# A transformer layer with experts on one core: when the second phase's first weights are sent for, and where ScalarE sends for second weights

## The reference

```
h   = gelu(x @ w1[e] + b1[e])        # 256 -> 1024, for every expert e
eo  = h @ w2[e] + b2[e]              # 1024 -> 256
out = sum over the 2 experts chosen for each token, weighted
```

## Time and profile before

| what | value |
|---|---|
| median of 3 runs | 795.15 us (794.45 to 796.68) |
| profiled execution, whole time | 792.84 us |
| its span, first to last instruction | 791.1 us |
| mean granted TensorE clock in it | 0.974 |
| TensorE busy | 740.1 us, 94% of the span |
| VectorE, ScalarE, GpSimd busy | 51%, 48%, 30% |

### The profile page before, as it was taken

The page is one execution under the profiler, slowest core; times in us unless marked ns, Lnnn a source line. Parts: engine busy times, 40 slices in busy tenths (PEclk is TensorE's granted clock), DMA queues, the critical chain, the costliest instruction groups (busy, mean ns, idle before and its releaser), DMA issues. The chain is left out here.

```text
span 791.1 us, 14690 instructions
## 1 busy us (share of the span) xinstructions
PE 740.1 (94%) x5275; PEld 504.9 (64%) x5275; DVE 402.5 (51%) x974; ACT 380.0 (48%) x776; POOL 238.3 (30%) x432
## 2 busy tenths in 40 slices
PE   6889999999999999999997799996999999999983
PEld 4444544555455545545663677895899999999931
DVE  4577777767666777565677453664111011011125
ACT  3325456655656657587753456332433333433303
POOL 8313400112353322424643153202222222222115
PEclk9999999999999999999997899998999999999998
DMA  8968200702046112323227826568699999999663
GB/s 273 289 163 233 83 1 4 201 3 83 1 121 203 49 19 59 106 74 109 56 109 243 263 89 237 179 215 299 187 322 336 331 318 321 344 323 316 200 209 124
DMA packets 95152, 140.29 MB, mean 177 GB/s; under 512 B 11855, under 2 KB 81077, under 8 KB 92597
## 3 DMA queue, kind: packets, MB, share of 16 engines
q1 hardware_dynamic: 78533, 109.95, 44.1%
q10 hardware_dynamic: 12896, 19.92, 7.4%
q0 software_dynamic: 3648, 9.45, 3.3%
HBM read 110.65 MB, written 28.65 MB: 176 GB/s over the span
## 5 line engine op out<-in xcount | busy, mean ns | idle before, releaser
L1450 DVE TENSOR_REDUCE neg_part_max<-work 128x1 f32<-128x512 f32 (+4 forms) x368 | 212.8, 625 | 79.1 <-PE work L906 40.0
L1220 ACT ACTIVATE arena<-score_pair 128x1024 f32<-128x1024 f32 (+2 forms) x224 | 179.8, 839 | 86.6 <-PE score_pair L939 51.0
L906 PE MATMUL work<-arena 96*128 96x77 bf16 (+4 forms) x640 | 119.2, 280 | 9.1 <-DVE neg_part_max L1450 3.0
L936 PE MATMUL score_pair<-arena 99*128 99x512 bf16 (+2 forms) x448 | 113.4, 336 | 0.0
L959 PE MATMUL out_acc<-arena 128*32 128x512 f32 (+4 forms) x896 | 107.3, 517 | 0.6 <-ACT arena L1232 0.5
L829 PE MATMUL score_pair<-arena 128*128 128x256 f32 x432 | 97.6, 379 | 0.0
L1380 DVE TENSOR_TENSOR arena<-score_pair,arena 128x256 f32<-128x256 f32 x27 | 11.5, 425 | 166.8 <-PE score_pair L829 164.2
L906 PEld LDWEIGHTS work<-arena 96*128 96x128 bf16 x640 | 49.8, 100 | 72.6 <-issue 35.4
L1860 POOL DMA_INDIRECT chosen_scratch<-arena,scatter_rows x36 | 35.5, 986 | 186.4 <-DVE arena L1382 183.6
L829 PEld LDWEIGHTS score_pair<-arena 128*128 128x128 f32 x432 | 80.1, 190 | 9.8
L823 PE MATMUL work<-arena 128*128 128x128 f32 x704 | 84.7, 279 | 0.5 <-ACT arena L1153 0.5
(11 more groups left out here) (263 smaller groups left out, 928.7 us busy)
## 6 DMA issues: line engine op xcount, KB each, us to landing
arena<-in_L_xattn_e_w SPq DMA_DIRECT2D x54, 1024.0 KB, 6.2
arena<-parts_scratch SPq DMA_DIRECT2D x24, 768.0 KB, 6.1
arena<-in_L_xattn_e_w ACTq DMA_DIRECT2D x18, 1024.0 KB, 5.8
parts_scratch<-arena_more SPq DMA_DIRECT2D x24, 384.0 KB, 3.2
parts_scratch<-arena_more SPq DMA_DIRECT2D x24, 256.0 KB, 3.4
arena<-chosen_scratch SPq DMA_DIRECT2D x16, 256.0 KB, 5.8
parts_scratch<-arena_more SPq DMA_DIRECT2D x24, 128.0 KB, 3.4
residual<-in_x SPq DMA_DIRECT2D x4, 512.0 KB, 7.9
```

The costliest lines, as they stand in the source:

```text
L906: m = pe.matmul(bank[:, j * it.w:(j + 1) * it.w], qa[st.half(it.g)][0:R_S, h, n0:n0 + P], k, start=True, stop=not it.last)
L936: m = pe.matmul(st2[pair][0:rows, j, 0:w], k, qa[st.half(it.g)][0:R_M, h, skip:QG], start=True, stop=not diagonal)
L1220: act_e.activation(pt[buf][0:rows, :, 0:w], st2[pair][0:rows, :, 0:w], ACT.Exp, scale=float(HD) ** -0.5).then_inc(pair_taken[pair], 1)
L1450: dve.tensor_reduce(pm[:, it.at, it.t, it.h0:it.h0 + it.nh], bank[:, 0:it.nh * it.w].rearrange("p (j k) -> p j k", j=it.nh), AX.X, ALU.max ...
```

## The change

Two edits. On ScalarE, at `t_up`, the wait for TensorE's product (`full`) now stands behind the wait for the second weights' buffer and the sending for `w2` of slot t, where it stood ahead of both. On SP, a wait for the landing of the first phase's last second weights, w2(8), now stands ahead of the sending for w1(9).

```diff
                 elif it.kind == "t_up":
-                    e.wait_ge(full[it.bank], it.use)
                     if it.t >= 2:
                         e.wait_ge(*down_done(it.t - 2))
                     if it.at == 0 and it.t >= RING2:
                         weights2(it.t)
+                    e.wait_ge(full[it.bank], it.use)
                     e.wait_ge(taken[b1_turned.bank], b1_turned.use)
                     half_gelu(it.t, it.at, bank).then_inc(taken[it.bank], 1)
@@
             e.wait_ge(ej_ok, 2)
             n_reg = sp.value_load(n_used[0:1, 0:1], min_val=NSURE, max_val=NSLOT)
+
+            e.wait_ge(*weights2_in(NFIRST - 1))
             weights1(NFIRST)
             for j in range(NFIRST, NSLOT):
```

## The result

The changed kernel took 786.88 us (median of 6 runs, 785.26 to 789.07) against 793.63 us for the kernel before over its 6 runs. The ratio is 0.9912, with a 95% interval of 0.9888 to 0.9937. A second sample of the same changed kernel gave 0.9934 (0.9910 to 0.9958), which is 5.2 us. The 95% intervals of the two overlap. One execution of the kernel before, beside the experiments, took 950.4 us at a mean clock of 0.744; it is left out of all ratios and means.

A forecast was written before the change was run, and what follows sets the result against it. TensorE, busy 94% of 791.1 us, bounds the kernel, so only its idle or half-clock time counts. A 6.65 us gain less 1.60 for the clock is 5.05, taken from 795.15: 790.1 us, range 787.4 to 792.6.

The forecast's parts named there:

- What was late: TensorE before down(8): its 6.9 us wait at L829 was for w2(8), 12.8 us in flight beside w1(9) and w1(10).
- ScalarE's edit: At up(8), w2(8) goes out 1.7 us sooner; slots 2 to 7 gain 0, bounds 0 and 0.5 us.
- SP's edit: w2(8), running alone, lands in 5.5 to 6.2 us; w1(9), sent some 5 us later, lands by 546.5, 2.8 us in hand.
- What is late next: Behind down(8): VectorE's bank read after three `w_split` passes sets turn(9) at 548.11 and up(9) at 549.26, shift 6.65 us.
- The clock: TensorE's half-clock stretch moves from down(8) to up(9), costing 1.60 us again; bounds 0 and 3.2.
- The base: Whole kernel before the change: median 795.15 us, from which the 5.05 us was taken; its profiled execution took 792.84.
- the forecast shift: Whole kernel: -6.65 us at up(9) plus 1.60 for the clock, -5.05 us, carried one to one to the end.
- The clock that stays up: TensorE at up(9): the shorter gap causes no clock fall, shift 6.65, 788.5 us; chance 0.13.
- VectorE out of the way: Behind down(8): passes end sooner or the bank read comes first, shift 8.5, 786.6 to 788.2 us; chance 0.05.
- w2(8) slow for another reason: Before down(8): GpSimd's gathers and scatters keep w2(8) at 12.8 us, 1.5 to 3 gained, 792.2 to 793.7; chance 0.11.
- nothing: Whole kernel: w2(8) wasn't held by the two first weights and the rest evens out, 795.2 us; chance 0.05.
- slower: Before up(9): SP's five delayed transfers land together, w1(9) at 555.5 to 556.5 or near 558, 796.7 to 799.2; chance 0.06.

## Why the prediction was right, and where it was wrong

- *What was late.* Right. w2(8) was held by what SP sent beside it, and TensorE's wait for it is gone. Beside the two first weights that were w2(9) and w1(11), which the prediction left out. It took 12.8 us with SP's transfers beside it, 8.7 with one first weight and 5.7 with none. What I set against the rival, that the other second weights took 5.5 to 6.2, holds for w2(2) to w2(7) only: w2(0) and w2(1), sent among the first phase's opening transfers, took 7.7 and 11.0.
- *ScalarE's edit: sends w2(8) 1.7 us sooner, and nothing for slots 2 to 7.* The numbers were right (0.06 us for slots 2 to 7). What I made of them was not: a lead of 1.7 us removes the whole wait by itself, so the two edits do the same thing twice. The prediction credited SP's wait alone with it. Nothing in the sum hung on that.
- *SP's edit.* Right: w2(8) in 5.7 us (5.5 to 6.2 forecast), w1(9) in 4.9 (4.8 to 6.0), and no up or down waits for weights. Those behind landed later than the 552, 555 and 558 that I had: w2(9) at 553.4, w1(11) at 557.5, w2(10) at 560.6. Nothing waited for them.
- *What is late next.* Right, and the step that mattered. Turn(9) 10.49 us behind down(7), forecast 548.11 - 537.50 = 10.61. The shift was 6.56 for 6.65. Moving `w_split` showed the cause.
- *The clock: the term of the sum that failed.* I took one fall of 1.60 us in the kernel before and "the same 1.6 us" in the changed one, so that the clock changed nothing between them. What the clock costs in a trace is what down(8) takes over 3.72 us and what the way from turn(9) to up(10) takes over the 4.94 of the trace with `w_split` moved. In the kernel before that is 1.6, 1.7 and 1.8 us in three traces and 4.4 and 4.1 in the two with a second fall, 2.7 on average. In the changed kernel it is 2.3, 2.3 and 1.6, 2.1 on average. So the clock gave back 0.66 us where I had 0. Over all traces the stretch from down(7) to up(10) went from a mean of 23.15 us (five) to one of 17.49 (three), a gain of 5.66, between 4.3 and 7.7 for a pair. Less the clock's 0.66 it is 5.00, against the 5.05 of the forecast.
- *The base: the larger error, of the same sign.* I took 5.05 from 795.15, the median of three executions. The 46 later ones have a mean of 793.8, 1.4 us less. From there even the forecast shift gives 788.7, and the same range, 1.4 us lower, would hold 786.88. The profiled execution's 792.84 was a hint that I put aside.
- *What the 3.2 us between 790.1 and 786.88 are made of.* The base is 1.4. The gain between the means of the 46 and the 14 executions is 6.2 instead of 5.05: 0.6 of that is the clock in the stretch, and for the other 0.6 no trace shows a place. The last 0.7 is the first sample, which lies below the 787.5 of both samples together; that is chance. (Each is rounded.)
- *The rivals.* The clock that stays up was not seen in the changed kernel; it came with `w_split` moved. VectorE out of the way, w2(8) slow for another reason, nothing and slower are all excluded by the traces. (The slower rival's 5.63 MB at 363 to 384 GB/s are 14.7 to 15.5 us, not 15 to 16, which changes nothing.)

Open: why the clock falls a second time in some executions of the kernel before and not in others at the same code; and how the DMA engines divide between the two queues. w1(10), w2(9) and w1(11) together cost w2(8) some 4 us (8.7 against 12.8) although they were sent 1.1 us and more after it, but with a lead of 1.7 us over w1(9) and 2.9 over w1(10) it landed in at most 7.5. No run here holds back w2(9) and w1(11) alone, and none tells which rule of sharing gives both numbers. So the turns packet by packet that the prediction took from the Trainium skill ("DMA: Bandwidth & Descriptors", section "Queues, rings and completion order") are neither shown nor refuted. What set the time ahead of down(0), 460 to 464 us in the traces, was not looked into; no edit touches it.

## What to carry to other kernels

When a long wait goes, ask of every engine what it did inside that wait: here VectorE's table passes had been hidden by it and took back 2 us directly and 2.3 through the clock, and moving them behind the urgent read gave nearly as much again as the change (4.3 us of the stretch). Here a transfer needed next, sent 1.7 us ahead of those needed later, needed no wait between them. Where a term of the sum is a clock fall, read it in several executions or keep it as a range, and compare kernels by stretches between fixed steps. And take the time before from more than three executions when the shift is of the size of their scatter: here the base was the larger error.

## What was unexpected of the hardware

A transfer of 1 MB took 12.8 us when it was sent 0.07 us behind one of 1 MB from another queue, with a second sent 1.1 us after it and two more before it had landed. It took at most 7.5 when it was sent 1.7 us ahead of the first. And the stretch from up(10) to the end came out within 0.1 us of 231.4 in twelve of the fourteen traces, with seven different kernels. Most of the scatter of whole times lies ahead of down(0), where the granted clock from 420 to 440 us was 0.66 to 0.75, by trace; that the clock makes the scatter there is not shown.
